# A deformable-convolution sampling loop: TensorE's next word and VectorE's slot and row registers are read earlier

## The reference, cut to what matters

```python
loc_y = ys + ky + offset[..., 1]
loc_x = xs + kx + offset[..., 0]
sampled = _bilinear_gather(value, loc_y, loc_x)
out = (sampled * mask[..., None]).sum(axis=4)
return out.reshape(N, L, C) @ Wo
```

## Time and profile before

| | |
|---|---|
| median of 3 runs | 1282.53 us |
| the profiled execution's own time | 1285.17 us |
| its span, first to last instruction | 1283.4 us |
| PE busy | 1035.7 us (81%) |
| DVE busy | 965.0 us (75%) |
| ACT busy | 398.9 us (31%) |
| tap products on DVE (L1403) | 516, 323.1 us |
| weighed products on DVE (L1436) | 600, 372.4 us |

### The profile page before, as it was taken

How to read it: one execution, slowest core, us unless ns; L and a number is a source line. 1 busy time by engine, 2 the same in 40 slices (tenths; PEclk the granted TensorE clock), 3 DMA queues, 4 the chain that set the end, 5 groups by cost and what they waited for, 6 DMA issues and landing times.

```text
span 1283.4 us, 24836 instructions
## 1 busy us (share of the span) xinstructions
PE 1035.7 (81%) x5436; PEld 403.7 (31%) x5437; DVE 965.0 (75%) x1657; ACT 398.9 (31%) x540; POOL 23.1 (2%) x35
## 2 busy tenths in 40 slices
PE   4997782599798879799742998979897998789874
PEld 3446661122232222232230332322222232223253
DVE  4656467588699768788874889868977888878863
ACT  3532332611404241311037304431324015520121
POOL 6000000000000000000000000000000000000000
PEclk8997775699799879899865999979998999999996
DMA  7800002002101210201111012310121012301111
GB/s 136 320 1 1 1 2 60 11 18 55 37 18 37 54 37 18 55 0 37 37 34 37 19 34 56 75 37 18 37 54 37 19 36 55 91 19 34 34 24 33
DMA packets 37585, 55.15 MB, mean 43 GB/s; under 512 B 16971, under 2 KB 18323, under 8 KB 37396
## 3 DMA queue, kind: packets, MB, share of 16 engines
q1 hardware_dynamic: 35268, 42.28, 14.2%
q0 software_dynamic: 2256, 12.17, 2.8%
HBM read 41.02 MB, written 13.39 MB: 42 GB/s over the span
## 4 chain that ended last, share of the span: by engine, by line
PE 64%; issue 11%; DVE 10%; DVEq 9%; ACT 3%; ACTq 1%; DMA 1%; POOL 0%; POOLq 0%
PE psA L1104 20%; PE T L1114 13%; PE psW L1114 13%; PE psA L704 6%; PE psA L1095 3%; DVE arena L1403 2%; DVE arena L1436 2%; DVEq L387 2%; DVE arena L1288 2%; PE psA L658 1%; ACT arena L1176 1%; ACTq L416 1%; DVEq L1436 1%; DVEq L1403 1%; DMA arena<-in_convw 1%
## 5 line engine op out<-in xcount | busy, mean ns | idle before, releaser
L1403 DVE TENSOR_TENSOR arena<-arena 128x512 f32 x516 | 323.1, 687 | 127.7 <-PE psA L1104 70.6
L1436 DVE TENSOR_TENSOR arena<-arena,psA 128x512 f32 x600 | 372.4, 682 | 34.9 <-issue 21.5
L1176 ACT ACTIVATE arena<-arena,cst 128x576 f32<-128x576 f32 (+2 forms) x236 | 167.1, 765 | 643.8 <-DVE arena L1403 588.6
L1104 PE MATMUL psA<-arena,cst 64*64 64x512 f32 x2064 | 333.9, 628 | 21.2 <-DVE arena L1403 20.2
L1114 PE MATMUL psW<-arena,cst 128*64 128x512 f32 x632 | 221.8, 659 | 32.3 <-DVE arena L1436 32.2
L1114 PE MATMUL T<-arena,cst 128*64 128x512 f32 x568 | 193.9, 654 | 23.4 <-DVE arena L1436 23.1
L1104 PEld LDWEIGHTS psA<-arena,cst 64*64 64x64 f32 x2064 | 117.8, 137 | 231.2 <-issue 226.7
L1181 ACT ACTIVATE arena<-arena 128x1152 f32<-128x1152 f32 (+1 forms) x94 | 132.4, 1409 | 5.9
L1114 PEld LDWEIGHTS psW<-arena,cst 128*64 128x64 f32 x632 | 64.3, 142 | 184.9 <-DVE arena L1436 178.0
L1095 PE MATMUL psA<-arena,cst 64*64 64x512 f32 x464 | 68.8, 662 | 61.4 <-issue 61.4
L1114 PEld LDWEIGHTS T<-arena,cst 128*64 128x64 f32 x568 | 58.0, 141 | 157.4 <-DVE arena L1436 151.2
(11 more groups left out here) (215 smaller groups left out, 535.8 us busy)
## 6 DMA issues: line engine op xcount, KB each, us to landing
arena<-planes SPq DMA_DIRECT2D x124, 284.0 KB, 4.1
planes<-arena POOLq DMA_DIRECT2D x1, 10000.0 KB, 29.3
planes<-arena SPq DMA_DIRECT2D x4, 512.0 KB, 5.1
arena<-in_convw POOLq DMA_DIRECT2D x4, 472.0 KB, 9.4
X<-in_x SPq DMA_DIRECT2D x8, 128.0 KB, 10.7
out_x<-X SPq DMA_DIRECT2D x16, 64.0 KB, 1.8
cst<-in_consts SPq DMA_DIRECT2D x1, 528.0 KB, 5.0
arena<-in_w SPq DMA_DIRECT2D x8, 64.0 KB
```

The lines of the kernel that those rows point to most:

```text
L1104: mm = pe.matmul(psA[64 * h:64 * h + 64, at:at + BANK], ident[rows, rows], Pt[rows, i, h], start=False, stop=True, skip_group_check=True, ...
L1176: act.activation(dst[:, i], src, ACT.Abs, bias=const("shift")[:, bass.ds(at + i, 1)]).then_inc(hat_abs, 1)
L1403: dve.tensor_tensor(Pt[:, i, h].rearrange("p (s y) -> p s y", s=SPAN), along_y, along_x.broadcast_to([128, SPAN, HW]), ALU.mult).then_inc( ...
L1436: dve.tensor_tensor(Mt[:, i, h].rearrange("p (y c) -> p y c", c=CG), v.rearrange("p (y c) -> p y c", c=CG), w.rearrange("p (y c) -> p y c" ...
```

## The change

On TensorE, `sums` no longer reads its unit's word at its head. It takes what is in the register, and reads the next unit's word inside its loop of products, after the matmuls of product (0, 1), so once per pair of taps. The word of the layer's first unit is read ahead of the loops.

On VectorE the slots of a tap pair are worked out by `slots_of` into two registers per buffer. It is called at the end of `fetch_list` (in the body of the `weigh` loop) for a unit's first pair, and at the end of each iteration of `weights` for the next pair. The row count and first row are worked out by `rows_of_unit`, called in each iteration of `weights` after product (1, 0) for the unit to be weighed next, and once after the masks, and no longer at the head of `weigh`. Two shifted views of `hy` and `ax` replace an addition of HW to the first slot, and the counter `hats` is raised after the loop, not before.

```diff
+        hys = [area(8960 + at, 2 * HY) for at in (HW, 0)]
+        axs = [area(19200 + at, 4 * SLOTS * HW).rearrange("p (b j t) -> p b j t", b=2, j=2) for at in (HW, 0)]
...
-            def sums(at, b):
-
-                word = unit_word(pe, regs, at)
+            def sums(b, next_at):
+
+                word = pe.snap(regs["word"], min_val=0, max_val=(1 << 23) - 1)
...
                         mm.then_inc(w_sum, 1)
+                        if (i, h) == (0, 1):
+                            unit_word(pe, regs, next_at)
...
+            unit_word(pe, regs, 0)
...
                     here = ic + g * MAX_SPANS
-                    sums(here, 0)
+                    after = next_spans(pe, regs, g, ic, nc_)
+                    sums(0, here + UNIT)
                     with pe.Fori(1, m) as i:
-                        sums((i * 2 - 1) * UNIT + here, 1)
+                        sums(1, i * 2 * UNIT + here)
                         accumulate(g, 0)
-                        sums(i * 2 * UNIT + here, 0)
+                        sums(0, i * 2 * UNIT + UNIT + here)
                         accumulate(g, 1)
-                    sums((m * 2 - 1) * UNIT + here, 1)
+                    sums(1, after)
...
+            def slots_of(w, b):
+                hold(dve, (w & 15) * HW, 0, (K - 1) * HW, reg=regs[f"first{b}"])
+                hold(dve, (w >> 4 & 15) * HW, 0, K * HW, reg=regs[f"second{b}"])
+
             def fetch_list(b):
...
                 tap_pairs(dve, word, regs[f"pairs{b}"])
+                slots_of(dve.snap(regs[f"list{b}"], min_val=0, max_val=(1 << 31) - 1), b)
...
+            def rows_of_unit(b):
+                word = dve.snap(regs[f"word{b}"], min_val=0, max_val=(1 << 23) - 1)
+                row_pairs(dve, word, regs["bound"])
+                hold(dve, word >> 20 & 7, 0, SPAN - 2, reg=regs["step"])
+
             def weights(b, rows_at, next_at):
 
-                dve.reg_add(regs["hats"], regs["hats"], 1)
-                dve.wait_ge(ax_ready, dve.snap(regs["hats"]))
+                dve.wait_ge(ax_ready, dve.snap(regs["hats"]) + 1)
                 dve.sem_inc(dve_turn, 1)
                 with dve.Fori(0, dve.snap(regs[f"pairs{b}"], min_val=1, max_val=5)):
-                    w = dve.snap(regs[f"list{b}"], min_val=0, max_val=(1 << 31) - 1)
-                    slots = (hold(dve, (w & 15) * HW + HW, 0, K * HW, reg=regs["slot0"]),
-                             hold(dve, (w >> 4 & 15) * HW, 0, K * HW, reg=regs["slot1"]))
+                    slots = (dve.snap(regs[f"first{b}"], min_val=0, max_val=(K - 1) * HW),
+                             dve.snap(regs[f"second{b}"], min_val=0, max_val=K * HW))
...
                             unit_word(dve, regs, next_at, f"next{1 - b}")
-                    dve.reg_mov(regs[f"list{b}"], w >> 8)
+                        elif (i, h) == (1, 0):
+                            rows_of_unit(1 - b)
+                    dve.reg_mov(regs[f"list{b}"], dve.snap(regs[f"list{b}"], min_val=0, max_val=(1 << 31) - 1) >> 8)
+                    slots_of(dve.snap(regs[f"list{b}"], min_val=0, max_val=(1 << 23) - 1), b)
                     dve.reg_add(regs["taps"], regs["taps"], 4)
+                dve.reg_add(regs["hats"], regs["hats"], 1)
...
             def weigh(b):
 
-                word = dve.snap(regs[f"word{b}"], min_val=0, max_val=(1 << 23) - 1)
-                row_pairs(dve, word, regs["bound"])
-                hold(dve, word >> 20 & 7, 0, SPAN - 2, reg=regs["step"])
                 take_next(b)
...
                     dve.sem_inc(dve_turn, 1)
+                    rows_of_unit(1)
                     weigh(1)
```

More of the change, by code:

```diff
@@ L1385, in fetch_list @@
                 tap_pairs(dve, word, regs[f"pairs{b}"])
+                slots_of(dve.snap(regs[f"list{b}"], min_val=0, max_val=(1 << 31) - 1), b)
             def take_next(b):
                 dve.reg_mov(regs[f"word{b}"], dve.snap(regs[f"next{b}"]))
+            def rows_of_unit(b):
+                word = dve.snap(regs[f"word{b}"], min_val=0, max_val=(1 << 23) - 1)
+                row_pairs(dve, word, regs["bound"])
+                hold(dve, word >> 20 & 7, 0, SPAN - 2, reg=regs["step"])
             def weights(b, rows_at, next_at):
-                dve.reg_add(regs["hats"], regs["hats"], 1)
-                dve.wait_ge(ax_ready, dve.snap(regs["hats"]))
+                dve.wait_ge(ax_ready, dve.snap(regs["hats"]) + 1)
                 dve.sem_inc(dve_turn, 1)
                 with dve.Fori(0, dve.snap(regs[f"pairs{b}"], min_val=1, max_val=5)):
-                    w = dve.snap(regs[f"list{b}"], min_val=0, max_val=(1 << 31) - 1)
-                    slots = (hold(dve, (w & 15) * HW + HW, 0, K * HW, reg=regs["slot0"]),
-                             hold(dve, (w >> 4 & 15) * HW, 0, K * HW, reg=regs["slot1"]))
+                    slots = (dve.snap(regs[f"first{b}"], min_val=0, max_val=(K - 1) * HW),
+                             dve.snap(regs[f"second{b}"], min_val=0, max_val=K * HW))
                     for i, h in itertools.product(range(2), range(2)):
-                        along_y = hy[:, bass.ds(rows_at, HY)].rearrange("p (s t) -> p s t", s=SPAN)[:, :, bass.ds(slots[i], HW)]
-                        along_x = ax[:, b, h:h + 1, bass.ds(slots[i], HW)]
+                        along_y = hys[i][:, bass.ds(rows_at, HY)].rearrange("p (s t) -> p s t", s=SPAN)[:, :, bass.ds(slots[i], HW)]
+                        along_x = axs[i][:, b, h:h + 1, bass.ds(slots[i], HW)]
                         dve.wait_ge(w_sum, dve.snap(regs["taps"]) + (2 * i + h + 1))
@@ L1518, in _ @@
             pe.wait_ge(ln_cst_in, 16)
-            regs = registers(pe, "taps", "steps", "units", "word", "pairs", "rows0", "rows1")
+            regs = registers(pe, "taps", "steps", "word", "pairs", "rows0", "rows1", "more", "after")
             ln_pe(pe, 0, X, x_loaded)
@@ L1551, in _ @@
             regs = registers(dve, "taps", "steps", "hats", "spans", "loads", "word0", "word1", "next0", "next1", "list0", "list1", "pairs0",
-                             "pairs1", "slot0", "slot1", "step", "bound", "more", "after", "next_g")
+                             "pairs1", "first0", "first1", "second0", "second1", "step", "bound", "more", "after", "next_g")
             for top, bot in A + B + D:
```

## The result

The changed kernel takes 1420.05 us in the median of 4 runs (1413.55 to 1421.9), against 1282.4 before; the ratio is 1.107, 95% interval 1.1035 to 1.1104. The profiled execution took 1413.55 us itself, the lowest of the four, with a span of 1411.7 us: +128.3 us against the span of before. TensorE's granted clock is 0.910 on the mean, not lower than before.

What follows compares the result with a forecast made beforehand. VectorE's sequencer, doing register work between products, was taken to bound the loops. Terms -23 + 28 + 37 + 67 + 5 - 7 gave +107 us on 1285.2, so 1392, or 1390 for the runs' median; range 1318 to 1432.

Steps and rivals of the forecast that it cites:

- the slots' terms: Slots' arithmetic moved to the list fetch and tap-pair ends: heads -16 to -23, tails +28, weigh iterations +25 and +42.
- step 6: TensorE's word read leaves the head of `sums`: -7 us at 8 group starts; its reads in the product loop cost 0.
- Step 4: Weigh loop, slots added to `fetch_list`: +25 us in units' first iterations, +42 us in the 92 later ones.
- Step 1: Head of a unit on VectorE: slots leave, two moves replace one, at 44 heads: -23 us.
- Step 2: End of tap-pair iterations: slots unused in each unit's last, +25 us before weigh loops, +3 at span starts; elsewhere unchanged.
- step 5: Tap loop on VectorE: two extra moves per later tap-pair iteration, +5 us (0 to 10).
- Step 3: Row count and first step in all 129 tap-pair iterations: +34 us for 71 extra turns, +3 at span starts.
- A: Rival: in-loop register work is hidden beside the products, faster by 30 us, 1252; chance 0.06.
- B: Rival: TensorE is the bound, all 61.4 us before its clears are won, 1221; chance 0.02.
- C: Rival: later weigh iterations have 0.35 us to spare, rows half covered, registers packed better: +50 us, 1333; chance 0.17.
- D: Rival: costs and gains cancel because fused register instructions absorb the moves, 1282; chance 0.03.
- E: Rival: TensorE's granted clock stands at 1.2 GHz for longer, +90 us on top, 1480; chance 0.03.

Runs made afterwards that it cites:

- e1_pe_only: Only the change's TensorE edits, VectorE as before, against the kernel before: 1282.08 us, ratio 0.9996.
- e5_after_slots_twice: The changed kernel with `slots_of` done twice in `fetch_list`: 1491.21 us, ratio 1.1628 to the kernel before.
- e14_pe_ranges_once: Kernel before plus the change's TensorE part, all groups' limits read once ahead of TensorE's loops, `next_spans` behind the first `sums`: 1258.68 us, ratio 0.9801.
- e2: Only the slots' part of the change, with the shifted views, against the kernel before: 1388.78 us, ratio 1.0826.
- e3: Only the row counts' part of the change, against the kernel before: 1310.34 us, ratio 1.0202.
- e4_reads_once: Kernel before with the next unit's word read once behind the tap loop and `fetch_list` once behind the weigh loop: 1284.67 us, ratio 1.0007.
- e9: Kernel before with the word's read behind the tap loop and the next pair's slots worked out in its old place: 1311.3 us, ratio 1.0219.
- e15: Kernel before with e14_pe_ranges_once's TensorE edits, VectorE's word read once behind the tap loop, and the shifted views: 1262.53 us, ratio 0.9831.

## Why the prediction was right

The way was right, and so was the mechanism of the loss: 1390 forecast, 1420 measured; +107 us by the sum, +128.3 in the spans of the profiled executions. That the size came out so near is in part luck, because errors of opposite sign met: the slots' terms were some 30 us too small (75 expected of them, 106 measured alone), the rows' term 10 us too large (37 against 27), and the 7 us of the group starts did not come. To compare step by step I took the start of every product in both traces and summed what lies beyond 0.60 us from the product before, by its place:

| place (step) | forecast | measured |
|---|---|---|
| first tap product after a weigh loop, 44 (1) | -23 | 42.4 to 26.9: -15.5 |
| first weighed product after tap products, 46 (2) | +25 | 23.0 to 52.4: +29.4 |
| first tap product of a later iteration, 83, span starts among them (2, 3, 5, 6) | +38 | 80.9 to 114.9: +34.0 |
| third and fourth tap product, 129 each | 0 | 3.4 to 20.2: +16.8 |
| third weighed product, first iteration, 58 (4) | +25 | 12.0 to 37.5: +25.5 |
| third weighed product, later iterations, 92 (4) | +42 | 7.6 to 50.3: +42.7 |

- The main reading held: VectorE's sequencer sets the pace inside the loops, and the chain's 64% for TensorE was misleading. The removal of TensorE's word read from every head gained nothing (e1_pe_only), the dose on the sequencer cost its full price (e5_after_slots_twice). At the starts of groups TensorE's own sequencer sets the pace: e14_pe_ranges_once won 25 us there, where step 6 saw 7.
- Step 4, the largest, was right in both halves.
- Step 1 was too large by 7.5 us. The cause is argued only: the sequencer used to enter the head with some lead from the weigh loop, and now comes late.
- Step 2 said that the slots, moved round the loop's corner, cost the same as before, and step 5 allowed 0.07 us a turn for the moves. That was too little: the slots' part alone makes the 83 later starts 14.5 us later. The trace of the changed kernel shows a move of 123 ns at the top of each tap pair (L1411), where it was 36 ns (L1396), and the counter's addition by itself, 59 ns (L1425), where one instruction had done it with the list's shift (L1407).
- Step 3 charged 0.48 us to each of 71 turns, +34. The rows' part alone makes the later starts 25.3 us later. It also said there was cover for the rows between the third and fourth product. The fours of 2.69 us show that there was not quite: the slots' part alone gives +7.4 us in those places by the same count, the rows' part alone +4.9, both together +16.8.
- Step 6 had -7 us for the starts of groups; e1_pe_only shows 0, because `next_spans`, which the term left out, took the read's place ahead of the clears.
- Of the marks set out beforehand, idle at the head (0.1 us), before weighed products (1.0) and the 16 products (12 us) came as said; the fours went to 3.44 us, above 3.25 to 3.35. TensorE's idle ahead of the clears fell from 61.4 to 39.5 us, 0.68 a unit on the mean and not 0.2: nearly all of it stands at the starts of groups and layers, which the mark did not set apart.
- The rivals: A and B are refuted by e1, e2 and e3; C by the later weigh iterations, which showed 0.46 us each; D by the result itself; E by the clock, 0.910 against 0.891.
- The step behind the sum was too plain. "What a place adds to the sequencer is time" is right where no lead is left, as in the loops of the changed kernel. "What an iteration saves is time won" is not: e4_reads_once took 0.60 us out of each tap pair and its later turns won 0.15 us each, and in e4, e9 and e15 the reads that stood behind the loops instead cost about as much or more. How much a piece costs depends on its place. The word's read after product (0, 1) was nearly covered; the rows' 0.48 us after product (1, 0), also under a running product but behind that read, was not, and cost 27 us.

The median lies 137.6 us above, the profiled spans 128.3; the changed kernel's four runs spread over 8.4 us, and I did not find why.

## What to carry to other kernels

Where an engine's instructions are 0.6 us long and their trip counts live in registers, sum the sequencer's work place by place: from the hand-over of one product to that of the next. An idle time that the profile gives to the partner engine, while that partner itself stands idle, is a sequencer's: here the waiting engine's own inside the loops, the partner's at the starts of groups. The recorded instructions of both sequencers in that stretch tell which. Moving register work "inside the loop" multiplies it by the trip count and adds it to the last, useless turn. Look for one-time reads in front of a stage's first instruction on the other engine: together with a moved `next_spans` they were worth 25 us here, more than any rearrangement in the loops.

## What the runs showed that I had not expected

- Register writes whose results are unused, or that repeat a value, did not appear in the trace at all (24008 instructions in five kernels), while the doubled `slots_of` behind a table read did (27874 against 26890). A dose of register work has to be checked by the instruction count before it is read.
- Taking a read of about 0.6 us out of each tap-pair iteration left 0.36 us of idle at its turn, and put 0.42 and 0.38 us of idle into the sequencer itself. The engine's idle fell below what the timeline shows only when the work at the corner itself was moved (e9_slots_mid).
